# Row-norm roots in small steps on two engines, a new instruction order, and five norm tiles of eight on GpSimd

## What is computed

```python
mod = (_silu(L0_c) @ L0_wmod).reshape(8, 6, 1, -1)         # sa, ca, ga, sb, cb, gb
h = _layernorm(x) * (1 + ca) + sa                           # the front
for i in range(6):                                          # DEPTH layers on h
    xn = _layernorm(h, ln1_w[i], ln1_b[i])                  # first norm
    q, k, v = xn @ wq[i], xn @ wk[i], xn @ wv[i]            # 8 heads of 16
    q = softmax(q, over the 16 columns of a head); k = softmax(k, over the rows)
    h = (q @ (k.T @ v)) @ wo[i] + bo[i] + h                 # linear attention
    xn = _layernorm(h, ln2_w[i], ln2_b[i])                  # second norm
    h = leaky_relu(xn @ w1[i]) @ w2[i] + h                  # 128 -> 512 -> 128
x = x + ga * h
h = _layernorm(x) * (1 + cb) + sb
x = x + gb * fp4_linear(silu(fp4_linear(h, w_gate)) * fp4_linear(h, w_up), w_down)
```

## Time and profile before

| | |
|---|---|
| median of 3 runs | 1197.98 us (1197.91 to 1198.08) |
| the profiled execution, span | 1196.8 us, first to last instruction |
| granted clock of PE, mean | 0.984 of full |
| PE busy | 1129.7 us (94%) |
| POOL busy | 1090.7 us (91%) |
| DVE busy | 1074.1 us (90%) |
| ACT busy | 1035.2 us (86%) |
| chain that ended last | POOL 34%, PE 27%, issue 22%, DVE 10% |

### The profile page before, as it was taken

One profiled execution on the slowest core, in us unless ns is written; L12 is line 12 of the kernel. 1 busy time (PEld: TensorE's weight loads), 2 busy tenths in 40 slices (PEclk: granted clock), 3 DMA queues, 4 the chain that ended last, 5 costly groups with the idle time before them and its releaser, 6 DMA issues.

```text
span 1196.8 us, 28581 instructions
## 1 busy us (share of the span) xinstructions
PE 1129.7 (94%) x9722; PEld 864.8 (72%) x9722; DVE 1074.1 (90%) x2885; ACT 1035.2 (86%) x1776; POOL 1090.7 (91%) x920
## 2 busy tenths in 40 slices
PE   7787999999999999999999999999999888999996
PEld 5574687787777777777778778777777755565664
DVE  7889889999999999999999999999987479999973
ACT  5687999999999999999999999999998795767753
POOL 4888999999999999999999999999999888999762
PEclk8799999999999999999999999999999999999998
DMA  8121778768778777687777776866767420110000
GB/s 308 36 71 53 214 213 217 188 209 219 179 205 217 194 216 189 193 221 177 219 212 182 224 202 190 220 194 194 214 188 217 107 61 21 44 37 36 19 19 36
DMA packets 213857, 190.13 MB, mean 159 GB/s; under 512 B 113392, under 2 KB 192080, under 8 KB 213712
## 3 DMA queue, kind: packets, MB, share of 16 engines
q1 hardware_dynamic: 213712, 188.31, 56.3%
HBM read 87.06 MB, written 76.02 MB: 136 GB/s over the span
## 4 chain that ended last, share of the span: by engine, by line
POOL 34%; PE 27%; issue 22%; DVE 10%; ACT 3%; DMA 2%; SPq 2%; DVEq 0%; POOLq 0%; ACTq 0%
POOL hidden L1787 15%; POOL rows_split L1779 6%; POOL arena L1760 4%; POOL arena L1793 3%; PE pair_mlp L576 2%; PE pair_mlp L556 2%; PE ring_pair L615 2%; PE ring_pair L616 2%; PE ring_pair L617 2%; PE pair L567 2%; PE pair L599 2%; DVE ring_pair L1371 2%; DVE arena L1508 2%; PE pair_mlp L674 1%; DVE arena L1389 1%
## 5 line engine op out<-in xcount | busy, mean ns | idle before, releaser
L1787 POOL TENSOR_TENSOR hidden<-hidden 128x2048 f16<-128x2048 f32 x92 | 376.1, 4088 | 0.0
L883 ACT ACTIVATE hidden<-ring_pair,hidden_bias 128x512 f32<-128x512 f32 x384 | 245.6, 686 | 27.9 <-PE ring_pair L617 27.5
L892 ACT ACTIVATE hidden<-hidden 128x2048 f16<-128x2048 f32 x96 | 183.4, 1911 | 17.8 <-PE mlp L633 15.6
L1100 DVE BATCH_NORM_STATS2 bn<-x_all 128x6 f32<-128x128 f32 x896 | 184.2, 278 | 3.2 <-POOL x_all L1739 1.9
L1713 POOL TENSOR_TENSOR rstd<-ve,minus_half 128x8 f32<-128x8 f32 x104 | 170.5, 1640 | 0.0
L852 ACT ACTIVATE arena<-x_all,nmr,rstd 128x128 f32<-128x128 f32 x384 | 157.9, 495 | 0.0
L615 PE MATMUL ring_pair<-arena,halves 128*128 128x512 f16 x384 | 146.1, 381 | 4.5 <-DMA arena<-rows_split 2.8
L616 PE MATMUL ring_pair<-arena,halves 128*128 128x512 f16 x384 | 146.0, 380 | 0.0
L617 PE MATMUL ring_pair<-arena,halves 128*128 128x512 f16 x384 | 145.9, 380 | 0.0
L631 PE MATMUL mlp<-halves,hidden 128*128 128x128 f16 x768 | 135.9, 219 | 1.4 <-POOL hidden L1787 1.4
L633 PE MATMUL pair_mlp<-halves,hidden 128*128 128x128 f16 x768 | 136.5, 220 | 0.0
(11 more groups left out here) (206 smaller groups left out, 3145.1 us busy)
## 6 DMA issues: line engine op xcount, KB each, us to landing
n_away<-all_blocks SPq DMA_DIRECT2D x47, 512.0 KB, 3.3
norm_raw<-n_away SPq DMA_DIRECT2D x188, 128.0 KB, 3.0
k_away<-all_blocks SPq DMA_DIRECT2D x45, 512.0 KB, 2.8
q_away<-all_blocks SPq DMA_DIRECT2D x45, 512.0 KB, 3.3
arena<-k_away SPq DMA_DIRECT2D x180, 128.0 KB, 3.6
arena<-q_away SPq DMA_DIRECT2D x180, 128.0 KB, 3.6
x_all<-in_L_attn_x SPq DMA_DIRECT2D x8, 512.0 KB, 5.4
x_in<-in_L_attn_x SPq DMA_DIRECT2D x8, 512.0 KB, 4.0
```

What stands on the lines that cost most here:

```text
L883: act.activation(hidden_t[:, c * W + h * HALF:c * W + (h + 1) * HALF], ring[n % 2], ACT.Prelu, bias=hidden_bias[:, b:b + 1], scale=HIDDEN_ ...
L892: act.activation(half_rows(hidden_hi, h), half_rows(hidden_t, h), ACT.Copy).then_inc(hidden_hi_ready, 1)
L1100: last = nc.vector.bn_stats(bn[:, 6 * t:6 * t + 6], src(t))
L1787: pool.tensor_tensor(half_rows(hidden_lo, h), half_rows(hidden_t, h), half_rows(hidden_hi, h), ALU.subtract).then_inc(hidden_lo_ready, 1)
```

## The change

1. The two roots of an item, on POOL with a power each, become one root per iteration for two norms: the first norm of item v and the second of item v - 4 (LAG = 4), on one 128x16 tile of moments, mv12. ACT makes a guess y = exp(-0.5 ln(variance + eps)), POOL makes one Newton step from it in small operations. The roots have two buffers each (v % 2). ACT loads a table set by name at its start.
2. The root of both norms now carries the factor 2^7 that only the second had; the first layer norm's weight is divided by it once (ln_cols).
3. POOL_TILES is 5 instead of 3, so ACT normalises 3 first-norm tiles.
4. The lists of all engines are in a new order, and with new offsets. The fillers (keep_warm) are gone. product_k waits for the biased context of the item before. The front, the weights' preparation and the first feed-forward units have other places. The lists after items(v) are unchanged.

```diff
-    POOL_TILES = 3
+    POOL_TILES = 5
...
             def product_k(i):
                 pe.wait_ge(norm1_t_ready, i + 1)
+                after(pe, ctx_o_ready, i - 1)
...
+            act.preload_act_table_set("natural_log_exp_and_others")
...
+            def root_guess(v):
+                after(act, mv1_ready, min(v + 1, ITEMS))
+                after(act, mv2_ready, min(v - LAG + 1, ITEMS))
+                after(act, root_steps, rooted(v - 1, SQUARED))
+                mv = mv12[:, :].rearrange("p (t k) -> p t k", k=2)
+                act.activation(root_log[:, :], mv[:, :, 1], ACT.Ln, bias=eps_cols[:, 0:1]).then_inc(root_log_ready, 1)
+                act.wait_ge(root_log_ready, v + 1)
+                after(act, root_steps, rooted(v - 1, ROOTED))
+                act.activation(root_y[:, :], root_log[:, :], ACT.Exp, scale=-0.5).then_inc(root_y_ready, 1)
...
             def moments1(i):
-                after(dve, rstd1_ready, i)
-                moments(bn1, mv1, bn1_done, mv1_ready, i)
+                after(dve, root_steps, rooted(i - 1, OPENED))
+                after(dve, root_log_ready, i)
+                moments(bn1, mv12[:, 0:2 * T], bn1_done, mv1_ready, i)
...
+            def root_open(v):
+                after(pool, mv1_ready, min(v + 1, ITEMS))
+                after(pool, mv2_ready, min(v - LAG + 1, ITEMS))
+                after(pool, root_steps, rooted(v - 1))
+                pool.tensor_scalar(root_ve[:, :], mv[:, :, 1], 1.0, LN_EPS, ALU.mult, ALU.add)
+                pool.tensor_scalar(root_shift[:, :], mv[:, :, 0], -1.0, 0.0, ALU.mult, ALU.add).then_inc(root_steps, 1)
+            def root_square(v):
+                pool.wait_ge(root_y_ready, v + 1)
+                pool.tensor_tensor(root_a[:, :], root_y[:, :], root_y[:, :], ALU.mult).then_inc(root_steps, 1)
+            def root_scale(v):
+                pool.tensor_tensor(root_r[:, :], root_a[:, :], root_ve[:, :], ALU.mult).then_inc(root_steps, 1)
+            def root_newton(v):
+                pool.tensor_scalar(root_r[:, :], root_r[:, :], -0.5 * ROW_SIZE, 1.5 * ROW_SIZE, ALU.mult, ALU.add).then_inc(root_steps, 1)
+            def root_done(v):
+                after(pool, norm1_ready, min(v - 1, ITEMS))
+                after(pool, norm1_rest_ready, min(v - 1, ITEMS))
+                after(pool, norm2_ready, v - 1 - LAG)
+                pool.tensor_tensor(rstd12[v % 2][:, :], root_r[:, :], root_y[:, :], ALU.mult).then_inc(root_steps, 1)
+            def root_offset(v):
+                pool.tensor_tensor(nmr12[v % 2][:, :], root_shift[:, :], rstd12[v % 2][:, :], ALU.mult).then_inc(root_steps, 1)
```

More of the change, by code:

```diff
@@ L514, in _ @@
             mlp0_bank = mlp[0]
-            filler = identity[:, :].bitcast(F16)
-            def keep_warm(bank, count, semaphore=None, value=0):
-                if semaphore is not None:
-                    pe.wait_ge(semaphore, value)
-                for n in range(count):
-                    nc.tensor.matmul(bank[:, 0:2 * P], filler[:, 0:P], filler, start=True, stop=True)
             def turn_first_n(i):
@@ L793, in _ @@
+                if v == 3: turn_first_k(2)
+                if on(v - 2): context(v - 2)
+                if v == 56: product_up(1, 1)
+                if on(v - 4): first_mlp(v - 4, 3)
+                if on(v - 5): second_mlp(v - 5, 3)
+                if v == 2: turn_first_k(1)
+                if on(v - 4): first_mlp(v - 4, 4)
+                if v == 52: product_gate(0, 2)
+            for v in range(ITEMS + 16):
                 items(v)
@@ L1071, in items @@
[L1071 to L1073 removed]
+                if v == 55: x_ties(1)
+                if v == 54: x_square(0)
+                if on(v - 5): exp_q(v - 5)
+                if on(v - 8): hidden_high(v - 8, 0)
+                if v == 59: gate(0, 3)
+                if v == 58: gate(0, 2)
+                if v == 54: x_hat(1)
+                if on(v - 4): first_norm_t(v - 4)
+                if v == 55: gate(0, 0)
+                if v == 7: copy_k(2)
@@ L1074, in _ @@
+                if v == 6: prepare_weights(1, range(3, DEPTH))
+            for v in range(ITEMS + 16):
                 items(v)
@@ new lines, in items @@
+                if v == 2: prepare_bounds()
+                if on(v - 4): mask_context(v - 4)
+                if v == 49: x_rows(0)
+                if v == 4: front_stats(7)
+                if v == 1: weight_bounds(1)
+                if v == 5: prepare_weights(0, range(3, DEPTH))
+                if v == 58: x_max(3)
+                if v == 3: output_bias()
+                if v == 58: hidden_tile(1, 1)
+                if v == 59: hidden_lift(0, 1)
+                if v == 55: x_scale(2)
@@ L1665, in _ @@
+                if v == 56: hidden_max(0)
+                if v == 2: front_stats(4)
+                if v == 1: weight_bounds(0)
+                if v == 56: x_lift(2)
+                if v == 54: x_scaled(2)
+                if v == 58: hidden_lift(0, 0)
+                if on(v - 4): add_attention(v - 4)
+                if v == 49: x_rows(1)
+            for v in range(ITEMS + 16):
                 items(v)
@@ new lines, in items @@
+                if v == 3: front_rows(2)
+                if v == 53: x_offset(0)
+                if v == 63: residual(3)
+                if v == 51: gate(1)
+                if on(v - 9): hidden_low(v - 9, 1)
+                if v == 49: gate(0)
+                if v == 54: x_root(1)
+                if v == 54: gate(3)
+                if v == 51: residual(1)
+                if v == 8: front_rows(7)
+                if v == 2: front_root(3)
+                if v == 53: residual(2)
+                if v == 54: x_divide(0)
@@ new lines, in items @@
+                if v == 6: front_rows(6)
+                if on(v - 7): second_norm_low(v - 7)
+                if v == 50: residual(0)
+                if v == 5: front_root(5)
+                if v == 51: gate(2)
+                if on(v - 3): normalise1(v - 3)
+                if v == 4: front_rows(3)
+                if v == 5: front_rows(4)
+                if on(v - 8): hidden_low(v - 8, 0)
+                if on(v - 5): normalise_q(v - 5)
+                if v == 5: front_root(6)
+                if rooting(v - 2): root_open(v - 2)
```

564 lines of the change are left out of this document (245 added, 319 removed).

## The result

The changed kernel takes 1224.5 us (median of 4 runs, 1223.1 to 1224.7), the kernel before beside it 1198.0; the ratio is 1.0208 [1.0194, 1.0223]. The forecast was 1193.0 us with a range to 1209. The profiled execution spans 1222.8 us, 26.0 more than before.

The account below looks back on a forecast made before the run. Prediction: PE, needing about 18.27 of 18.39 us per period, bounds the steady part, between a fill and a drain; 1196.8 - 4 + 2 - 3 = 1191.8 us of span, with 1.2 us on top 1193.0 us; range 1180 to 1209.

Parts of the forecast that it names:

- (a): Joint roots and moved tiles, steady part: POOL -2.1 us per item, ACT no change, worth at most 4.9 us.
- rival 4: The new roots make ACT change tables after all, twice per root: 1271 us; chance 3 in 100.
- Worth at most the 4.9 us: Steady part: savings on POOL and ACT lie beside PE's 18.27 us per period, so they gain at most 4.9 us.
- (b): New order in the steady part: the period becomes 18.27 us, -4 us in all (bounds -6 and +6).
- the third circle: Steady part, attend on PE through DVE's list and back to PE: 17.8 us, 18.3 with weight steps of 1.56 us.
- (c): The fill: -1.5 us from the order, +3.5 us from the clock, +2 us together (bounds -4 and +14).
- From there DVE is the pace: Fill, after PE's transposes begin 7.3 us late: DVE's unchanged sum of work sets the pace; -1.5 us.
- Its price of 3.5 us: Fill without the 172 fillers: PE's lower clock costs 3.5 us, as DVE work hides most half-rate parts.
- (d): Drain and start of the feed-forward stage: sooner roots and a new fetch order give -3 us (bounds -14 and +9).
- Rival 1: Cold fill: without fillers DVE waits for PE at 1.2 GHz in items 0 to 4; 1206 us; chance 18 in 100.
- Rival 2: Steady part: a stretched POOL operation delays the second norm, PE stalls 0.2 us per period; about 1202; chance 13 in 100.
- that of the second norm: Steady part, circle from ACT's second norm through POOL's rows_lo, tiles, hidden subtraction, normalise_q and root to ACT: 17.5 us.

Follow-up runs that it names:

- The experiment with the moved line: The changed kernel with the 18 gate steps moved on DVE from before max_k to before max_q: 1199.3 us, ratio 1.0006 to the kernel before.
- before_cold: The kernel before without its 172 filler matmuls, nothing else changed: 1197.0 us, ratio 0.9974.
- the repaired kernels: Versions of the changed kernel with the gate steps before max_q on DVE; that edit alone measured 1199.3 us, ratio 1.0006.
- ff_sooner: The changed kernel with the gate steps before max_q, and the feed-forward stage's unit 0 earlier on TensorE and ScalarE: 1202.2 us, ratio 1.0018.

## Why the prediction was wrong

**(a) Roots, right in size.** POOL's 105.18 us in 120 / 18.11 = 6.63 periods are 15.9 us per item (16.1 forecast); before, 116.63 us in 6.56 periods were 17.8. ACT's 114.36 are 17.3; its logarithm and exponential take 0.305 and 0.216 us on average. There are two table loads, so rival 4 falls. "Worth at most the 4.9 us" failed: it took PE's 18.27 us as fixed because its work is fixed. PE's own order was part of the change, and the period fell to 18.11.

**(b) The steady part, wrong, and the largest error.** The step that failed is "Only the weight steps of 1.56 us (instead of about 1.1 in most items) bring this to 18.3 us, for about six items", the inserted step of the third circle. The circle itself was nearly right: 17.8 us with 1.1 inserted is 16.7 without a step, where the runs show 16.98; with the 2.1 to 2.6 us that the gate steps took it gives 18.8 to 19.3, and 19.42 was measured. What failed was to take a duration from the old place to a new one. The trace held the warning: the earlier trace rows show a 0.20 us root operation at 0.69 (446.60 us), and I read it as GpSimd's trouble alone, though a rounding step ran on DVE just then, at twice and more the 0.70 us that the same step takes in the changed kernel:

```profile
445.68 1.56 DVE L1421 TENSOR_TENSOR f_w<-x_in,f_w 128x560 f32<-128x560 f32 x1
```

Effect: +23.5 us from 18 periods, against -11.5 us (41 x 0.28) from the shorter period; 12.7 in all with 0.7 from scattered longer periods, where I had -4. The experiment with the moved line took back 25 us.

**(c) The fill, wrong.** The start was right: POOL at the first norm at 42.37 us (42.4 forecast), the transposes at 44.60 (44.5), the first residual add at 83.2 (83). "The late start is made good by item 2" failed: the adds of items 1 to 3 came at 108.4, 130.9 and 149.2 us, not 103, 120 and 138; against before, all four adds are 8.4 to 9.1 us late. The step that failed is "From there DVE is the pace". Between 40 and 140 us DVE is busy for less of the time than before, not more, and the kernel before without its fillers has it busiest (after, before, before_cold):

```profile
40.00:140.00 100.00, 66.79 (x349) 49.79 (x350) 83.44 (x263) 71.13 (x137) 76.78 (x107) 0.77 0.21 69
40.00:140.00 100.00, 77.78 (x553) 60.49 (x552) 90.08 (x273) 79.29 (x146) 85.13 (x82) 0.93 0.28 88
40.00:140.00 100.00, 70.42 (x434) 53.40 (x433) 94.10 (x293) 82.02 (x151) 90.62 (x86) 0.81 0.34 103
```

In the changed order DVE waits, for 5.7 us in three waits on product_z and 3.1 us on one product_k among others, and every other engine is less busy too. The clock itself was foreseen about right: 0.77 between 40 and 140 us makes 46 us at the lower level, (1 - 0.77) / 0.5, an estimate. Its price of 3.5 us failed; taking the fillers away gained 0.26% in the kernel before, and adding them gave nothing in the time that came again. Measured +9.1 us in this execution, +5.6 to +6.6 in the repaired kernels with the same fill (item 5 at 147.5 to 148.5), against +2. Against the kernel before without fillers, whose two traces have item 5 at about 137 us, the new fill is 10 to 14 us late. What is left as the cause is the order of the engines' lists behind item 0, since a start 10 us sooner moved nothing; no run shows it for items 3 to 5, and which wait decides is open.

**(d) The drain, wrong in sign:** +4.2 us from item 46 on, not -3. The rows below are, before and after, attention's last residual add, the MLP's last one, the first gate product and the first output product:

```profile
951.64 1.22 DVE L1251 TENSOR_TENSOR x_all<-pair,x_all 128x1024 f32<-128x1024 f32 x1 [2.07 <-PE pair L599]
...
1007.73 0.75 DVE L1261 SCALAR_TENSOR_TENSOR x_all<-mlp,mlp_up,x_all 128x512 f32<-128x512 f32 x1
970.59 0.86 PE L669 MATMUL pair_mlp<-all_blocks,halves 128*128 128x352 f32 x2
1014.37 1.02 PE L694 MATMUL mlp<-x_all,identity 128*128 128x512 f32 x2
```
```profile
970.65 1.23 DVE L1262 TENSOR_TENSOR x_all<-pair,x_all 128x1024 f32<-128x1024 f32 x1 [4.05 <-PE pair L602]
...
1014.18 0.75 DVE L1272 SCALAR_TENSOR_TENSOR x_all<-mlp,mlp_up,x_all 128x512 f32<-128x512 f32 x1
1001.20 0.76 PE L672 MATMUL pair_mlp<-all_blocks,halves 128*128 128x352 f32 x2
1039.91 1.02 PE L697 MATMUL mlp<-x_all,identity 128*128 128x512 f32 x2
```

Counted from product_k of item 47 (914.94 and 937.22 us), attention ends 3.3 us sooner (33.4 instead of 36.7), which is the forecast's -3, though its source was read too large: PE waits 2.8 us for the load of the earlier trace rows, not 5. The step that failed is that nothing behind it would change, as the feed-forward units' "work is the same": from attention's end to the first output product it takes 69.3 us instead of 62.7. The MLP's last add comes 15.8 us sooner (77.0 instead of 92.8), but that is mostly an exchange: before, the first gate product stands ahead of item 47's first_mlp (at 55.7 and 56.9 us), after, behind it (at 64.0 and 56.2), and the first output comes at 102.7 instead of 99.4. From there to the end both kernels take the same (182.4 and 182.9 us). Moving unit 0 ahead again did not help (ff_sooner), so which wait costs the 6.6 us is open.

**Rivals.** Rival 1 (cold fill) falls with before_cold: no loss of 10.5 us, but a gain. Rival 2 (a circle does not close) has the right form, at 10 us in place of 23.5, but named another circle, that of the second norm. The outcome lay outside the range because the range's upper end of (b), +6, took a circle to miss by 0.25 us and not by 1.3; the fill's +9.1 and the drain's +4.2 lay within their own bounds, though not near what was expected. All three signs of being wrong came: a steady period of 19.42 us (over 18.4), item 5's product_k at 150.97 us (after 150), and the last residual of item 47 at 96.5 instead of 111.9 us after product_k of item 46 (over 5 us apart).

## What to carry to other kernels

A duration from a trace belongs to a place, not to an instruction: before you move a VectorE operation that reads two SBUF tensors, or a tensor_scalar from SBUF to SBUF, look at what GpSimd runs at its new time, since it may have to wait for all of it (here 0.38 us became 2.1 or 3.6). Put such operations beside GpSimd's small ones. And an engine's idle time in a closed circle of waits is mostly not slack: test it by adding a known cost there (1.64 us added, 1.1 us paid).

## What the runs showed of the hardware that was not expected

- A 128x512 tensor_scalar on VectorE took 0.38 us alone and up to 3.6 us beside one GpSimd operation of 4.09 us, with an end 0.28 us after that one's. It goes both ways: a GpSimd root operation of 0.22 us took mostly 0.55 to 0.62 us beside a step with two SBUF inputs and 0.30 beside a tensor_scalar. VectorE's reductions from PSUM (1.16 to 1.22 us), its stream transposes (1.19 to 1.25) and its adds with one PSUM operand (0.72 to 0.75) kept their times beside the same GpSimd work.
- A step that had waited 0.97 us under one GpSimd operation got in ahead of the next, which followed without a gap and was stretched from 0.20 to 0.38 us (at 520.96 us, before). A step whose record started 0.03 us ahead of the next GpSimd operation was held through all of that one (at 553.32 us, after).
- A group of fp32 128x128 matmuls behind short fp16 ones loses 0.055 us at its second matmul; behind a 128x512 matmul it does not. Three such places add up to the 0.16 us by which two periods of 18.27 and 18.11 us differ.
- TensorE at its lower clock level for part of the fill (granted clock 0.81 instead of 0.93 between 40 and 140 us) cost the kernel before no time that could be measured; without its 172 fillers it took about 3 us less (ratio 0.9958 to 0.9990).
